# C repeated by DMA instead of TensorE, and a scan that works in place in three PSUM banks

## Chip, cores and metric

The kernel runs on one core of a Trainium2 chip. The metric is the device time of one execution in microseconds. Three runs of the kernel before gave 3733.61, 3746.4 and 3751.59 us; the median is 3746.4.

## What is computed

x is [32, 512, 256] in fp32: 32 sequences of 512 tokens and 256 channels. A macaron block: half a feed-forward, a selective scan, half a feed-forward.

```python
x = x + 0.5 * ffn(layernorm(x), w_gate, w_up, w_down)
x = x + attn(layernorm(x), ...)
x = x + 0.5 * ffn(layernorm(x), w_gate, w_up, w_down)

def ffn(x, w_gate, w_up, w_down):          # 704 hidden; FP4 in blocks of 16, every operand
    return fp4_linear(silu(fp4_linear(x, w_gate)) * fp4_linear(x, w_up), w_down)

def attn(x, W_in, b_in, W_dt1, b_dt1, W_dt2, b_dt2, A, D):     # N = 16 states
    B, C = split(x @ W_in + b_in)
    dt = clip(softplus((x @ W_dt1 + b_dt1) @ W_dt2 + b_dt2), 1e-7, 1e6)
    tmp = A * dt[..., None]
    B_barX = expm1(tmp) / tmp * dt[..., None] * B[:, :, None, :] * x[..., None]
    _, h = associative_scan(combine, (exp(tmp), B_barX), axis=1)   # h = exp(tmp) h_before + B_barX
    return sum(h * C[:, :, None, :], axis=-1) + D * x
```

## The kernel before

Each engine's program is one loop over 34 iterations. Iteration `it` works on several sequences at once: stage A (first feed-forward) and R (norm, projections, dt) for sequence `it`, S (the scan) for `it-1`, C (second feed-forward) for `it-2`, N (norm and quantisation of the next input) for `it+1`. The order in which an engine does the pieces of these stages is a list written out by hand, `ORDER` (lines 27 to 62), with one list for each engine. A word such as `S.w7` is stage, piece and index. Every engine executes its list strictly in order and waits on semaphores in front of each piece, so a piece that waits holds up all that is behind it on its engine. One pass through a list is called a sequence here, and the place where the lists start anew is the seam.

The scan stage works with channels on the 128 partitions, in two groups (G = 2), and tokens along the 512 columns. For each of 16 states n and group gi there is one group m = 2n + gi, 32 in all:

- PE `w` (`differences`, L1303): 12 matmuls of 128x129 write x times the token-to-token differences of B into bank gi of `w_ps`. It waits for the scan that used this bank before.
- ACT `b` (L1103) and POOL `bl` (L495) make the differences of B, ACT `d` (L1115) makes the decay exp(A dt).
- DVE `g` (`state_of`, L787): `tensor_tensor_scan` reads `w_ps` and `decay` and writes `state` in SBUF.
- PE `c` (`repeat_c`, L1313): one matmul of 48x512 repeats row n of C over all 128 partitions into the bank `rep_ps`, from `C_parts`, which holds C as fp16 high part (ACT `ch`, L1067) and low part (DVE `sc`, L760) and is multiplied by a selection matrix `pick_row`.
- DVE `p` (`times_c`, L797): `state` (SBUF) times 1/A times `rep_ps` (PSUM) into `c_state`.
- PE `p` and `e` (`add_y`, L1323): 4 transposing matmuls add `c_state` to `y_ps`.

At the start of a sequence stand k0 and k1, the direct part: PE L1285 writes a product of B, C and D into `w_ps`, DVE L778 multiplies it by x. At the end DVE `y0` (L806) adds `y_ps` to the residual.

Of the feed-forwards these pieces matter: PE `gu` (L1229, 12 matmuls: gate and up), ACT `gu` (L1048, the gate's silu), DVE `hid` (L701, gate times up), DVE `qv` and POOL `qp` (the high and low fp16 parts of the quantised hidden layer), SP `ht` (L416, their transpose by DMA), PE `dn` (L1243, down), DVE `res` (L733, the residual). `N.qy0` and `N.qy1` on DVE (L690) make the next input's fp16 parts, SP `N.tx0` and `N.tx1` (L405) transpose them, and A.gu0 needs them. `R.dt0` (L770, L773) makes dt, `R.xl0` on POOL (L484) the low part of x. `R.cb0` (L752) multiplies B by C from PSUM; `R.rb0` (L1061) takes the projections rows B and C into `rBC`.

PSUM is full: two banks for gate/up, one for the down product, two for `y_ps`, two for `w_ps`, one for `rep_ps`. All DMAs are issued by SP on one queue, in its list's order.

## Time and profile before

| | |
|---|---|
| median of 3 runs | 3746.4 us |
| the profiled execution | 3731.64 us |
| its span, first to last instruction | 3729.6 us |
| mean granted clock of TensorE | 0.966 of full speed |
| busy: PE, DVE, ACT, POOL | 3292.7 (88%), 3399.4 (91%), 2999.9 (80%), 2873.4 us (77%) |
| DMA | 192.07 MB, mean 51 GB/s |

Busy shares are over the whole span. Of its first 200 us a large part goes to the quantisation of the weights and to filling the pipeline, so the work of one sequence is read from a window in the middle. Idle time of an engine in front of a group of instructions is given with what released it; a wait for several semaphores is put down to the one that came last.

### The profile page before, as it was taken

The page shows a single profiled execution, that of the slowest core. Times are in us where ns is not written, and L with a number is a line of the kernel's source. Part 1 is how long each engine was busy: PE and PEld are TensorE (multiplying, and loading weights), DVE is VectorE, ACT ScalarE, POOL GpSimd, SP SyncE. Part 2 cuts the span into 40 slices and gives each one's busy share as a digit, 9 for nine tenths or more (in the row PEclk, how much of TensorE's full clock was granted, in tenths as well). Part 3 has the DMA queues.
Part 4 walks back from the last instruction along what each step waited for, and adds up shares of the span by engine and source line. Part 5 has one row for each costly group of instructions (what it writes and reads, how often), then busy time and mean ns, then how long its engine had stood idle before and what let it go on. Part 6 is the DMA issues. An engine that isn't in the chain of part 4 may idle for free. (4 is left out here: it accounts for less than half of the span.)

```text
span 3729.6 us, 79626 instructions
## 1 busy us (share of the span) xinstructions
PE 3292.7 (88%) x28716; PEld 2351.3 (63%) x28716; DVE 3399.4 (91%) x5419; ACT 2999.9 (80%) x6314; POOL 2873.4 (77%) x2489
## 2 busy tenths in 40 slices
PE   0589999999998999999999999999999999999984
PEld 0256666666666666666666666666666666666663
DVE  5499999999999999999999999999999999999984
ACT  1388888888888888888888888888888888888872
POOL 2458788788877788787878878788888888888854
PEclk9799999999999999999999999999999999999987
DMA  2112222222222222222222222222222222232212
GB/s 37 25 33 49 52 52 54 58 60 46 59 49 51 54 63 47 55 55 49 55 58 61 45 59 49 54 53 60 50 55 60 49 55 54 58 63 43 53 35 43
DMA packets 583023, 192.07 MB, mean 51 GB/s; under 512 B 544039, under 2 KB 578280, under 8 KB 582632
## 3 DMA queue, kind: packets, MB, share of 16 engines
q1 hardware_dynamic: 582632, 186.98, 24.3%
q8 instruction: 230, 3.77, 0.4%
q14 instruction: 161, 1.32, 0.1%
HBM read 19.16 MB, written 16.78 MB: 10 GB/s over the span
## 5 line engine op out<-in xcount | busy, mean ns | idle before, releaser
L787 DVE TENSOR_TENSOR_SCAN state<-w_ps,decay 128x512 f32<-128x512 f32 x1024 | 1210.6, 1208 | 60.3 <-PE w_ps L1303 56.5
L1229 PE MATMUL gu_ps<-wgu,qxT 128*128 128x352 f16 x6144 | 1032.6, 320 | 101.9 <-ACT gate L1048 51.4
L1303 PE MATMUL w_ps<-bdif,x_parts 128*128 128x129 f16 (+1 forms) x12288 | 850.3, 222 | 96.0 <-DVE state L787 88.5
L1303 PEld LDWEIGHTS w_ps<-bdif,x_parts 128*128 128x128 f16 x12288 | 754.0, 98 | 218.4 <-issue 175.3
L1229 PEld LDWEIGHTS gu_ps<-wgu,qxT 128*128 128x128 f16 x6144 | 577.1, 99 | 480.7 <-ACT gate L1048 65.3
L1115 ACT ACTIVATE decay<-dt,A_sb 128x512 f32<-128x512 f32 x1024 | 686.3, 711 | 71.0 <-DVE state L787 43.6
L797 DVE SCALAR_TENSOR_TENSOR c_state<-state,inv_A,rep_ps 128x512 f32<-128x512 f32 x1024 | 723.1, 738 | 7.7 <-issue 3.5
L495 POOL TENSOR_TENSOR bdif<-dif,B_lo 128x516 f16<-128x516 f16 x512 | 535.9, 1060 | 164.7 <-PE w_ps L1303 164.0
L1243 PE MATMUL dn_ps<-wd,qhT 128*128 128x256 f16 (+1 forms) x4608 | 591.6, 279 | 64.0 <-DMA qhT<-qh 62.5
L1323 PE MATMUL y_ps<-ident,c_state 128*128 128x128 f32 x4352 | 621.5, 279 | 22.7 <-DVE c_state L797 22.7
L1103 ACT ACTIVATE bdif<-dif,B_tok 128x129 f16<-128x129 f16 x2048 | 628.9, 393 | 0.0
L1243 PEld LDWEIGHTS dn_ps<-wd,qhT 128*128 128x128 f16 (+1 forms) x4608 | 424.2, 99 | 204.0 <-DMA qhT<-qh 80.3
L1323 PEld LDWEIGHTS y_ps<-ident,c_state 128*128 128x128 f32 x4352 | 470.2, 141 | 121.1 <-issue 81.5
L534 POOL TENSOR_TENSOR val<-val,magic 128x704 f32<-128x704 f32 x256 | 410.5, 1604 | 166.0 <-DVE magic L729 166.0
L1048 ACT ACTIVATE gate<-gu_ps,w_back 128x352 f32<-128x352 f32 x512 | 281.8, 550 | 300.9 <-PE gu_ps L1229 296.6
L542 POOL TENSOR_TENSOR grid<-val,magic 128x704 f16<-128x704 f32 x256 | 444.0, 1735 | 20.1
L526 POOL TENSOR_TENSOR val<-hid,recip 128x704 f32<-128x704 f32 x256 | 378.6, 1494 | 28.3 <-DVE recip L717 27.6
L701 DVE SCALAR_TENSOR_TENSOR hid<-gu_ps,up_back,gate 128x352 f32<-128x352 f32 x512 | 290.2, 567 | 81.2 <-PE gu_ps L1229 65.7
L557 POOL TENSOR_TENSOR qh<-grid,scale_lo 128x704 f16<-128x704 f16 x256 | 354.0, 1388 | 0.4
L1115 ACT ACT_TABLE_LOAD x188 | 241.2, 1283 | 3.3
L724 DVE TENSOR_TENSOR qh<-grid,scale_hi 128x704 f16<-128x704 f16 x256 | 240.7, 940 | 3.2 <-POOL grid L542 3.1
L1039 ACT ACTIVATE magic<-val 128x704 bf16<-128x704 f32 x256 | 197.3, 782 | 39.9 <-POOL val L526 36.0
(160 smaller groups left out, 3803.3 us busy)
## 6 DMA issues: line engine op xcount, KB each, us to landing
x_in<-in_L_attn_x SPq DMA_DIRECT2D x32, 512.0 KB, 3.8
x_s<-x_a SPq DMA_DIRECT2D x32, 512.0 KB, 3.8
out<-x_out SPq DMA_DIRECT2D x32, 512.0 KB, 3.2
qhT<-qh SPq DMA_TRANSPOSE x256, 3.7
qxT<-qx SPq DMA_TRANSPOSE x128, 3.1
hid<-in_L_ffn_w_gate SPq DMA_DIRECT2D x1, 704.0 KB
bdif<-in_L_ffn_w_up SPq DMA_DIRECT2D x1, 704.0 KB
val<-in_L_ffn_w_down SPq DMA_DIRECT2D x1, 704.0 KB, 13.1
```

The lines of the kernel that those rows point to most:

```text
L495: g.tensor_tensor(bdif[:, n % NB, :, 1, 0:P + 1], dif[:, 0:P + 1].unsqueeze(1).broadcast_to([P, T, P + 1]), B_lo[:, seq % 2, :, n:n + 1].b ...
L526: g.tensor_tensor(val[:, t % 2].rearrange("p (b i) -> p b i", i=BLOCK), hid[:, t, :].rearrange("p (b i) -> p b i", i=BLOCK), recip[:, t * ...
L534: g.tensor_tensor(val[:, s], val[:, s], magic[:, s], ALU.add).then_inc(grid_h.sem, 1)
L542: g.tensor_tensor(grid[:, s], val[:, s], magic[:, s], ALU.subtract).then_inc(grid_h.sem, 1)
L787: v.tensor_tensor_scan(state[:, n % 2, gi, :], w_ps[:, gi, :], decay[:, n % 2, gi, :], 0.0, ALU.add, ALU.mult).then_inc(state_ready.sem, 1)
L797: v.scalar_tensor_tensor(c_state[:, n % 2, gi, :], state[:, n % 2, gi, :], inv_A[:, gi, n:n + 1], rep_ps[:], ALU.mult, ALU.mult).then_inc( ...
L1103: last = a.activation(bdif[:, n % NB, t, 0, 0:P + 1], dif[:, 0:P + 1], ACT.Copy, scale=B_tok[:, seq % 2, t, n:n + 1])
L1115: a.activation(decay[:, n % 2, gi, :], dt[:, seq % 2, gi, :], ACT.Exp, scale=A_sb[:, gi, n:n + 1]).then_inc(decay_ready.sem, 1)
L1229: last = te.matmul(gu_ps[:, m, 0:FH], qxT[:, t // 2, 4 * (t % 2) + xp * G + c], wgu[:, c, wp, a:a + FH], start=begin, stop=end)
L1243: last = te.matmul(dn_ps[:], qhT[0:k, t % 2, hp * FC + c, :], wd[0:k, c, wp, :], start=begin, stop=end)
L1303: last = te.matmul(w_ps[:, gi, t * P:t * P + wide], x_parts[:, seq % 2, xp, t, gi * P:(gi + 1) * P], bdif[:, n % NB, t, bp, 0:wide], start ...
L1323: last = te.matmul(y_ps[:, t // 2, col:col + P], c_state[:, n % 2, gi, t * P:(t + 1) * P], ident[:], is_transpose=True, start=(j, t % 2) = ...
```

## The change

C no longer goes through TensorE. Once a sequence SP writes the rows of `rBC` that hold C (16 x 512, fp32) to a scratch in HBM (`C_rows`, two halves in turn), and eight DMAs (`cr0` to `cr7`) read two rows each of it back into all 128 partitions of `C_all` (512 KB each, 4 MB a sequence). `C_parts`, `pick_row`, `is_row`, `rep_ps` and the pieces PE `c`, ACT `ch`, DVE `sc` go. The bank that `rep_ps` held goes to `w_ps`, which has three banks used in turn by the two direct products and the 32 groups (34 uses a sequence). The scan writes its result over its input in the bank, and the product with C reads it from there; `state` goes. A bank is therefore free for PE when the product has been made, not when the scan has. The first product of each pair of states waits for its DMA. All five lists are reordered; of PE's and DVE's the new one is shown whole and of the old one the first and last line; SP's is whole. ScalarE's and GpSimd's are left out of the diff: in them R.xh0 (the fp16 high part of x) moves ahead of R.rb0 and of the softplus, and pieces change places within their stages.

```diff
     "PE": """
-    S.c0 S.k0 S.k1 A.gu0 S.w0 S.w1 S.e0 S.e1 S.w2 A.gu1 A.gu2 S.w3 S.c1 S.p0 S.p1 S.w4 S.w5 A.gu3 S.w6 S.w7 S.p2
...
-    S.w28 S.w29 S.c13 C.dn2 S.w30 S.c14 S.p24 S.p25 S.p26 S.p27 S.w31 S.c15 S.p28 C.dn3 S.p29 S.p30 S.p31
+    S.k0 S.k1 S.w0 S.w1 A.gu0 S.w2 S.w3 S.e0 A.gu1 S.w4 A.gu2 S.e1 S.p0 A.gu3 S.w5 S.w6 S.w7 S.p1 S.p2 S.p3
+    A.gu4 S.p4 S.p5 S.w8 S.w9 S.w10 A.gu5 A.gu6 S.p6 S.p7 A.gu7 C.gu0 S.p8 S.p9 S.w11 S.w12 S.w13 S.p10 C.gu1
+    A.dn0 S.w14 S.w15 S.w16 S.p11 S.p12 A.dn1 C.gu2 S.p13 C.gu3 S.w17 C.gu4 S.p14 S.p15 S.w18 A.dn2 S.w19 S.w20
+    C.gu5 A.dn3 S.w21 C.gu6 S.p16 S.p17 S.p18 C.gu7 S.w22 S.w23 S.p19 S.p20 S.p21 C.dn0 S.w24 S.w25 C.dn1 R.xt0
+    S.w26 S.p22 R.rb0 S.w27 S.w28 R.bt0 S.p23 S.p24 R.z0 C.dn2 S.w29 S.w30 S.w31 S.p25 S.p26 S.p27 S.p28 C.dn3
+    S.p29 S.p30 S.p31
     """,
     "DVE": """
-    S.k0 S.k1 S.g0 S.g1 S.p0 A.hid0 S.p1 C.xa0 C.xa1 A.hid1 C.xs0 A.am0 S.g2 A.hid2 S.g3 S.p2 S.g4 S.p3 C.xm0
...
-    C.res2 S.g29 S.p28 S.p29 S.g30 S.g31 N.qy0 S.p30 S.p31 C.res3 R.dt0 N.qy1 S.y0
+    S.k0 S.k1 S.g0 S.g1 S.p0 S.p1 S.g2 A.hid0 C.xa0 C.xa1 C.xs0 S.g3 A.hid1 C.xm0 A.am0 S.g4 S.p2 A.hid2 S.p3
+    S.p4 C.qy0 A.hid3 C.xm1 A.am1 A.qs0 S.g5 S.g6 S.p5 S.g7 S.p6 S.p7 C.qy1 S.g8 A.hid4 A.qm0 A.qm1 S.g9 A.hid5
+    S.p8 S.p9 S.g10 A.hid6 A.qv0 S.p10 A.hid7 A.am2 A.am3 A.qv1 A.qs1 C.hid0 S.g11 S.g12 S.g13 S.p11 A.qm2 S.p12
+    S.p13 A.qm3 A.res0 S.g14 S.g15 A.qv2 C.hid1 S.p14 S.p15 A.res1 C.hid2 C.am0 S.g16 C.hid3 C.am1 S.g17 C.qs0
+    A.qv3 S.p16 S.p17 C.hid4 C.qm0 A.res2 S.g18 C.qm1 S.p18 S.g19 S.g20 C.hid5 A.res3 S.g21 C.am2 S.p19 S.p20
+    S.p21 C.hid6 C.qv0 C.qv1 C.hid7 C.am3 C.qs1 S.g22 S.g23 S.p22 C.res0 C.qm2 S.g24 S.g25 S.p23 S.p24 C.res1
+    N.xa0 N.xa1 N.xs0 C.qm3 C.qv2 S.p25 S.g26 S.g27 R.tb0 R.cb0 S.g28 S.p26 S.p27 S.p28 C.qv3 N.xm0 N.xm1 S.g29
+    C.res2 S.g30 S.g31 S.p29 S.p30 S.p31 C.res3 R.dt0 N.qy0 N.qy1 S.y0
     """,
...
     "SP": """
-    S.keep0 C.tx0 C.tx1 A.ht0 A.ht1 A.ht2 A.ht3 N.load0 C.ht0 C.ht1 C.ht2 C.ht3 N.tx0 N.tx1 C.store0
+    S.keep0 C.tx0 C.tx1 S.cr5 S.cr6 A.ht0 A.ht1 A.ht2 A.ht3 N.load0 C.ht0 C.ht1 S.cr7 C.ht2 C.ht3 R.cw0 C.store0
+    N.tx0 N.tx1 R.cr0 R.cr1 R.cr2 R.cr3 R.cr4
     """,
...
     PR = ROW_C + N
-    KC = 3 * N
     NB = 4
+    BANKS = 3
...
         y_ps = psum("y_ps", [P, G, L])
-        w_ps = psum("w_ps", [P, 2, L])
-        rep_ps = psum("rep_ps", [P, L])
+        w_ps = psum("w_ps", [P, BANKS, L])
...
         B_lo = sb("B_lo", [P, 2, T, N], F16)
-        C_parts = sb("C_parts", [P, 2, L], F16)
+        C_all = sb("C_all", [P, N, L])
+        C_rows = nc.dram_tensor("C_rows", [2, N, L], F32, kind="Internal").ap()
         CB = sb("CB", [ROW_B + N + 1, L])
         rBC = sb("rBC", [PR, L])
         soft = sb("soft", [P, G, L])
         dt = sb("dt", [P, 2, G, L])
         bdif = sb("bdif", [P, NB, T, 2, WIDE], F16)
         decay = sb("decay", [P, 2, G, L])
-        state = sb("state", [P, 2, G, L])
         c_state = sb("c_state", [P, 2, G, L])
         consts_in = count("consts_in")
...
         dt_ready = count("dt_ready", G + 1)
-        rep_full = count("rep_full", N)
+        C_out = count("C_out", 16)
+        C_in = [count("C_in_%d" % k, 16) for k in range(N // 2)]
...
+        def w_bank(seq, u):
+
+            return w_ps[:, (seq * (G + G * N) + u) % BANKS, :]
+
         gu_flat = gu_ps[:].rearrange("p a b -> p (a b)")
         block = ctx.enter_context(nc.Block())
...
+            def keep_C(seq):
+
+                sp.wait_ge(r_ready.sem, r_ready.at(seq, 1))
+                if before(seq, 2):
+                    for k in range(N // 2):
+                        sp.wait_ge(C_in[k].sem, C_in[k].at(seq - 2, 16))
+                sp.dma_start(C_rows[seq % 2], rBC[ROW_C:PR, :]).then_inc(C_out.sem, 16)
+
+            def repeat_C(seq, k):
+
+                sp.wait_ge(C_out.sem, C_out.at(seq, 16))
+                if not first(seq):
+                    sp.wait_ge(c_state_ready.sem, c_state_ready.at(seq - 1, G + 2 * G * k + 2 * G))
+                sp.dma_start(C_all[:, 2 * k:2 * k + 2, :],
+                             C_rows[seq % 2, 2 * k:2 * k + 2, :].unsqueeze(0).broadcast_to([P, 2, L])
+                             ).then_inc(C_in[k].sem, 16)
+
             def body(it, pieces, pass_a, pass_c, pass_n):
                 q = {"A": pass_a, "C": pass_c, "N": pass_n}
                 for stage, step, k in pieces:
-                    if step == "tx":
+                    if step == "cw":
+                        keep_C(it)
+                    elif step == "cr" and stage == "R":
+                        repeat_C(it, k)
+                    elif step == "cr":
+                        repeat_C(it - 1, k)
+                    elif step == "tx":
                         turn_x(q[stage], k)
                     elif step == "ht":
                         turn_h(q[stage], k)
...
                 dve.wait_ge(w_ready.sem, w_ready.at(seq, gi + 1))
-                v.tensor_tensor(c_state[:, 1, gi, :], xT[:, gi, :], w_ps[:, gi, :], ALU.mult).then_inc(c_state_ready.sem, 1)
+                v.tensor_tensor(c_state[:, 1, gi, :], xT[:, gi, :], w_bank(seq, gi), ALU.mult).then_inc(c_state_ready.sem, 1)
             def state_of(seq, m):
                 n, gi = m // G, m % G
                 dve.wait_ge(decay_ready.sem, decay_ready.at(seq, m + 1))
-                if n >= 2:
-                    dve.wait_ge(c_state_ready.sem, c_state_ready.at(seq, m - G + 1))
                 dve.wait_ge(w_ready.sem, w_ready.at(seq, G + m + 1))
-                v.tensor_tensor_scan(state[:, n % 2, gi, :], w_ps[:, gi, :], decay[:, n % 2, gi, :], 0.0,
+                v.tensor_tensor_scan(w_bank(seq, G + m), w_bank(seq, G + m), decay[:, n % 2, gi, :], 0.0,
                                      ALU.add, ALU.mult).then_inc(state_ready.sem, 1)
             def times_c(seq, m):
...
                 if gi == 0:
-                    dve.wait_ge(rep_full.sem, rep_full.at(seq, n + 1))
+                    dve.wait_ge(C_in[n // 2].sem, C_in[n // 2].at(seq, 16))
                 dve.wait_ge(state_ready.sem, state_ready.at(seq, m + 1))
-                v.scalar_tensor_tensor(c_state[:, n % 2, gi, :], state[:, n % 2, gi, :], inv_A[:, gi, n:n + 1], rep_ps[:],
+                v.scalar_tensor_tensor(c_state[:, n % 2, gi, :], w_bank(seq, G + m), inv_A[:, gi, n:n + 1], C_all[:, n, :],
                                        ALU.mult, ALU.mult).then_inc(c_state_ready.sem, 1)
             def take_y(seq, pass_c):
...
                 act.wait_ge(rB_ps.sem, rB_ps.at(seq, 1))
+                if not first(seq):
+                    act.wait_ge(C_out.sem, C_out.at(seq - 1, 16))
                 a.activation(rBC[:], gu_ps[0:PR, 0, :], ACT.Identity, bias=b_rBC[0:PR, :]).then_inc(r_ready.sem, 1)
-
-            def high_C(seq):
-                act.wait_ge(rB_ps.sem, rB_ps.at(seq, 1))
-                if before(seq, 2):
-                    act.wait_ge(rep_full.sem, rep_full.at(seq - 2, N))
-                a.activation(C_parts[0:N, seq % 2, :], gu_ps[ROW_C:PR, 0, :], ACT.Identity,
-                             bias=b_C[0:N, :]).then_inc(C_hi.sem, 1)
             def softplus(seq):
...
                         pe.wait_ge(CB_ready.sem, CB_ready.at(seq, 1))
-                        pe.wait_ge(C_lo.sem, C_lo.at(seq, 1))
                     te.matmul(gu_ps[:, gi, :], W_dt2_sb[:, gi * P:(gi + 1) * P], rBC[0:R, :], start=True,
                               stop=True).then_inc(z_ps.sem, 1)
+            def bank_free(seq, u):
+
+                uses = seq * (G + G * N) + u - BANKS
+                if uses >= 0:
+                    pe.wait_ge(c_state_ready.sem, uses + 1)
+
             def direct(seq, gi):
                 if gi == 0:
                     pe.wait_ge(CB_ready.sem, CB_ready.at(seq, 1))
-                    if not first(seq):
-                        pe.wait_ge(state_ready.sem, state_ready.at(seq - 1, G * N))
-                te.matmul(w_ps[:, gi, :], AD[ROW_B:ROW_B + N + 1, gi * P:(gi + 1) * P], CB[ROW_B:ROW_B + N + 1, :], start=True,
+                bank_free(seq, gi)
+                te.matmul(w_bank(seq, gi), AD[ROW_B:ROW_B + N + 1, gi * P:(gi + 1) * P], CB[ROW_B:ROW_B + N + 1, :], start=True,
                           stop=True).then_inc(w_ready.sem, 1)
...
                     pe.wait_ge(x_lo.sem, x_lo.at(seq, 1))
                 pe.wait_ge(b_hi_ready.sem, b_hi_ready.at(seq, n + 1))
                 pe.wait_ge(b_lo_ready.sem, b_lo_ready.at(seq, n + 1))
-                if n:
-                    pe.wait_ge(state_ready.sem, state_ready.at(seq, m - G + 1))
-                else:
-                    pe.wait_ge(c_state_ready.sem, c_state_ready.at(seq, gi + 1))
+                bank_free(seq, G + m)
+                bank = w_bank(seq, G + m)
                 for t in range(T):
                     wide = P + (t < T - 1)
                     for xp, bp in PARTS:
-                        last = te.matmul(w_ps[:, gi, t * P:t * P + wide], x_parts[:, seq % 2, xp, t, gi * P:(gi + 1) * P],
+                        last = te.matmul(bank[:, t * P:t * P + wide], x_parts[:, seq % 2, xp, t, gi * P:(gi + 1) * P],
                                          bdif[:, n % NB, t, bp, 0:wide], start=(t, xp, bp) == (0, 0, 0),
                                          stop=(t, xp) == (T - 1, 1), skip_group_check=True)
                 last.then_inc(w_ready.sem, 1)
-
-            def repeat_c(seq, n):
-                if n:
-                    pe.wait_ge(c_state_ready.sem, c_state_ready.at(seq, G + G * n))
-                else:
-                    pe.wait_ge(C_lo.sem, C_lo.at(seq, 1))
-                te.matmul(rep_ps[:], pick_row[:, n, :], C_parts[0:KC, seq % 2, :], start=True, stop=True).then_inc(rep_full.sem, 1)
             def add_y(seq, j):
```

The prologue loses the making of `is_row` and `pick_row` (DVE), the clearing of `C_parts` (POOL) and two small loads; `w_val`, a buffer of the weights' quantisation, moves from `state` to `C_all`.

## Rows read from the trace of the kernel before

**Rows 1.** Busy time by engine, 400 to 3500 us: us (instructions), granted clock, DMA
```profile
core 0: us, PE busy (x) PEld busy (x) DVE busy (x) ACT busy (x) POOL busy (x), PEclk, DMA share, GB/s
400.00:3500.00 3100.00, 2878.18 (x25413) 2063.79 (x25412) 2934.53 (x4706) 2656.30 (x5584) 2530.89 (x2184) 0.98 0.26 54
```

**Rows 2.** Groups of instructions, 400 to 3500 us: busy, mean ns, idle before, releasers
```profile
L787 DVE TENSOR_TENSOR_SCAN state<-w_ps,decay 128x512 f32<-128x512 f32 x908 | 1073.4, 1208 | 50.5 <-PE w_ps L1303 48.4 <-ACT decay L1115 2.1
...
L1303 PE MATMUL w_ps<-bdif,x_parts 128*128 128x129 f16 (+1 forms) x10908 | 751.7, 222 | 79.3 <-DVE state L787 75.4 <-DVE c_state L778 3.8
...
L797 DVE SCALAR_TENSOR_TENSOR c_state<-state,inv_A,rep_ps 128x512 f32<-128x512 f32 x908 | 641.3, 738 | 5.7 <-issue 2.7 <-PE rep_ps L1313 1.7
...
L701 DVE SCALAR_TENSOR_TENSOR hid<-gu_ps,up_back,gate 128x352 f32<-128x352 f32 x457 | 258.9, 567 | 55.6 <-PE gu_ps L1229 40.5 <-ACT gate L1048 13.4 <-issue 0.2
...
L1313 PE MATMUL rep_ps<-C_parts,pick_row 48*128 48x512 f16 x453 | 177.0, 391 | 7.1 <-DVE c_state L797 7.1
...
L733 DVE SCALAR_TENSOR_TENSOR x_out<-dn_ps,down_back,x_c 128x256 f32<-128x256 f32 x112 | 53.3, 476 | 28.7 <-PE dn_ps L1243 28.5
...
L760 DVE SCALAR_TENSOR_TENSOR C_parts<-gu_ps,b_C,C_parts 16x512 f16<-16x512 f32 x28 | 21.1, 753 | 0.9
...
L773 DVE TENSOR_SCALAR dt<-dt 128x1024 f32<-128x1024 f32 x28 | 19.4, 694 | 1.0
```

**Rows 3.** Timeline of DVE around four seams: start, us, instruction, idle before
```profile
837.77 2.34 DVE L787 TENSOR_TENSOR_SCAN state<-w_ps,decay 128x512 f32<-128x512 f32 x2 [0.50 <-PE w_ps L1303]
...
945.40 2.34 DVE L787 TENSOR_TENSOR_SCAN state<-w_ps,decay 128x512 f32<-128x512 f32 x2 [0.50 <-PE w_ps L1303]
...
1045.85 2.07 DVE L690 TENSOR_TENSOR qx<-x_grid,x_scale_hi 128x512 f16<-128x512 f16 x1
...
1059.19 2.34 DVE L787 TENSOR_TENSOR_SCAN state<-w_ps,decay 128x512 f32<-128x512 f32 x2 [3.21 <-PE w_ps L1303]
...
1606.06 0.40 DVE L690 TENSOR_TENSOR qx<-x_grid,x_scale_hi 128x512 f16<-128x512 f16 x1
...
1611.02 0.42 DVE L806 SCALAR_TENSOR_TENSOR x_c<-y_ps,x_s 128x256 f32<-128x256 f32 x1
...
1614.17 2.34 DVE L787 TENSOR_TENSOR_SCAN state<-w_ps,decay 128x512 f32<-128x512 f32 x2 [0.50 <-PE w_ps L1303]
```

**Rows 4.** Timeline of PE around two seams, columns as in rows 3
```profile
1049.82 1.31 PE L1323 MATMUL y_ps<-ident,c_state 128*128 128x128 f32 x8 [2.03 <-DVE c_state L797]
...
1054.09 3.70 PE L1229 MATMUL gu_ps<-wgu,qxT 128*128 128x352 f16 x12
...
1610.99 1.96 PE L1229 MATMUL gu_ps<-wgu,qxT 128*128 128x352 f16 x12
```

**Rows 5.** Busy time by engine in a stretch at a slow seam, columns as in rows 1
```profile
1055.00:1060.00 5.00, 5.00 (x37) 3.72 (x36) 1.79 (x3) 4.81 (x12) 4.51 (x8) 0.57 0.77 247
```

**Rows 6.** Groups of instructions, whole span, columns as in rows 2
```profile
L778 DVE TENSOR_TENSOR c_state<-xT,w_ps 128x512 f32<-128x512 f32 x64 | 41.0, 680 | 0.7 <-PE w_ps L1285 0.7
...
L1076 ACT ACTIVATE soft<-gu_ps,b_dt_sb 128x512 f32<-128x512 f32 x64 | 40.5, 684 | 0.8
...
L1080 ACT ACTIVATE gu_ps<-gu_ps,b_dt_sb 128x512 f32<-128x512 f32 x64 | 39.7, 658 | 1.0
...
L910 DVE TENSOR_TENSOR state<-hid,recip 88x1024 f32<-88x1024 f32 x2 | 2.4, 1218 | 0.0
...
L910 DVE TENSOR_TENSOR state<-val,recip 128x704 f32<-128x704 f32 x2 | 1.7, 890 | 0.0
```

**Rows 7.** Timeline of SP's DMA issues at the seam, columns as in rows 3
```profile
1611.13 1.23 SPq L405 DMA_TRANSPOSE qxT<-qx  x1
```

**Rows 8.** DMA issues of the whole span: count, KB each, median us to landing
```profile
x_in<-in_L_attn_x SPq DMA_DIRECT2D x32, 512.0 KB, 3.8
...
b_C<-in_L_attn_b_in SPq DMA_DIRECT2D x3, 0.1 KB, 1.6
W_rBC<-in_L_attn_W_in SPq DMA_DIRECT2D x2, 16.0 KB, 2.1
...
b_in_all<-in_L_attn_b_in SPq DMA_DIRECT2D x1, 16.0 KB, 3.5
```

More of the change, by code:

```diff
@@ L28 @@
     "PE": """
-    S.c0 S.k0 S.k1 A.gu0 S.w0 S.w1 S.e0 S.e1 S.w2 A.gu1 A.gu2 S.w3 S.c1 S.p0 S.p1 S.w4 S.w5 A.gu3 S.w6 S.w7 S.p2
-    S.c2 A.gu4 A.gu5 S.c3 S.w8 S.p3 S.p4 S.w9 A.gu6 S.p5 S.c4 S.p6 A.gu7 C.gu0 S.w10 S.w11 S.p7 S.c5 S.p8 S.p9
-    S.w12 C.gu1 A.dn0 S.w13 C.gu2 S.c6 S.w14 S.w15 C.gu3 S.p10 A.dn1 C.gu4 S.w16 S.w17 S.p11 A.dn2 S.p12 C.gu5
-    S.c7 A.dn3 S.c8 S.p13 C.gu6 S.w18 C.gu7 S.c9 S.p14 S.w19 S.w20 S.p15 S.p16 S.p17 C.dn0 S.w21 S.w22 C.dn1
-    S.w23 S.c10 R.xt0 S.w24 S.w25 R.rb0 S.c11 S.p18 S.p19 R.bt0 S.p20 S.w26 S.c12 S.p21 S.w27 S.p22 S.p23 R.z0
@@ L35 @@
+    S.w26 S.p22 R.rb0 S.w27 S.w28 R.bt0 S.p23 S.p24 R.z0 C.dn2 S.w29 S.w30 S.w31 S.p25 S.p26 S.p27 S.p28 C.dn3
+    S.p29 S.p30 S.p31
     """,
     "DVE": """
-    S.k0 S.k1 S.g0 S.g1 S.p0 A.hid0 S.p1 C.xa0 C.xa1 A.hid1 C.xs0 A.am0 S.g2 A.hid2 S.g3 S.p2 S.g4 S.p3 C.xm0
-    S.g5 C.xm1 S.g6 A.hid3 A.am1 A.qs0 A.hid4 S.p4 S.p5 S.g7 A.hid5 C.qy0 C.qy1 A.qm0 A.qm1 S.p6 S.p7 S.g8 S.g9
-    A.hid6 S.p8 S.p9 A.hid7 A.am2 A.am3 A.qs1 A.qv0 S.g10 S.g11 C.hid0 S.p10 S.p11 A.qm2 A.qm3 S.g12 A.qv1
-    C.hid1 S.g13 C.am0 A.res0 A.qv2 C.hid2 S.p12 S.g14 S.g15 C.hid3 C.am1 A.res1 S.p13 C.qs0 A.qv3 S.g16 S.g17
@@ L41 @@
-    C.qm0 C.hid4 A.res2 C.qm1 C.hid5 S.p14 S.p15 C.am2 C.qv0 A.res3 C.hid6 S.p16 S.p17 S.g18 C.hid7 C.qv1 C.am3
-    C.qs1 S.g19 S.g20 C.res0 S.p18 S.p19 C.qm2 S.g21 S.g22 C.res1 S.g23 S.p20 S.p21 S.g24 S.g25 N.xa0 N.xa1
-    S.p22 S.p23 R.tb0 N.xs0 C.qm3 C.qv2 R.sc0 R.cb0 S.p24 S.g26 S.g27 S.p25 S.g28 S.p26 S.p27 C.qv3 N.xm0 N.xm1
-    C.res2 S.g29 S.p28 S.p29 S.g30 S.g31 N.qy0 S.p30 S.p31 C.res3 R.dt0 N.qy1 S.y0
+    S.k0 S.k1 S.g0 S.g1 S.p0 S.p1 S.g2 A.hid0 C.xa0 C.xa1 C.xs0 S.g3 A.hid1 C.xm0 A.am0 S.g4 S.p2 A.hid2 S.p3
@@ L298, in macaron_program @@
         r_ready = count("r_ready", 1)
-        C_hi = count("C_hi", 1)
-        C_lo = count("C_lo", 1)
         B_ps = count("B_ps", 1)
@@ L372, in _ @@
             sp.dma_start(b_rBC[ROW_C:PR, :], column(b_in[N:2 * N])).then_inc(bc_in.sem, 16)
-            for k in (0, 2 * N, ROW_B):
-                sp.dma_start(b_C[k:k + N, :], column(b_in[N:2 * N])).then_inc(bc_in.sem, 16)
+            sp.dma_start(b_C[ROW_B:ROW_B + N, :], column(b_in[N:2 * N])).then_inc(bc_in.sem, 16)
             sp.dma_start(W_dt2_sb[:], W_dt2).then_inc(consts_in.sem, 16)
@@ L820, in body @@
                         times_B(it)
-                    elif step == "sc":
-                        low_C(it)
                     elif step == "k":
@@ L882, in _ @@
             body(-1, order("DVE", "N"), None, None, 0)
-            w_val = state[:].rearrange("p a g l -> p (a g l)")
+            w_val = C_all[:, 0:2 * G, :].rearrange("p n l -> p (n l)")
             w_magic = decay[:].rearrange("p a g l -> p (a g l)").bitcast(BF16)
@@ L1143, in body @@
                         take_rBC(it)
-                    elif step == "ch":
-                        high_C(it)
                     elif step == "xh":
@@ L1343, in body @@
                         differences(seq, k)
-                    elif step == "c":
-                        repeat_c(seq, k)
                     elif step == "e":
```

49 lines of the change are left out of this document (18 added, 31 removed).

## The prediction

> **What bounds the kernel now.** I read first what each engine does between 400 and 3500 us, where the pipeline is full: VectorE (DVE) is busy 2934.5 of 3100 us (94.7%), TensorE (PE) 2878.2 (92.8%), ScalarE 86%, GpSimd 82% [rows 1]. Next the groups of instructions in that window. The `dt` clamp (L773) runs once a sequence and 28 times there, so a sequence takes 110.7 us: 104.8 of DVE work and 5.9 of DVE idle time, against 102.8 of PE work. DVE sets the pace, PE is close behind. A microsecond taken from DVE's work or idle time counts; one taken from PE counts only where DVE waits for PE.
>
> The last part of each line says what DVE waited for: 48.4 us for the differences in `w_ps`, 40.5 and 13.4 for the gate/up matmuls and the gate, 28.5 for the down matmuls, only 1.7 for the repeated C. PE in turn waits 75.4 us for scans to free a bank [rows 2].
>
> The 48.4 us lie at the seam between two sequences, and seams come in two kinds [rows 3]. At 1614.17 the first scan waited 0.50 us, at 1059.19 it waited 3.21. Of the 28 seams 9 wait 3.2 us or more, 5 wait 1.7 to 2.1, the rest 0.5 or less. A slow one begins on DVE: the N.qy0 instruction at 1045.85 takes 2.07 us where the one at 1606.06 takes 0.40. The products behind it are late and PE sits idle 2.03 us for them. Then 12 gate/up matmuls take 3.70 us, where 12 take 1.96 at the other seam [rows 4], and the granted clock of that stretch is 0.57, most of it at 1.2 instead of 2.4 GHz [rows 5]. The old list puts these 12 (A.gu0) ahead of w0 and w1.
>
> **The change, part by part, per sequence.**
>
> *C no longer by TensorE.* The `repeat_c` matmuls hold PE for 177.0 us [rows 2], 6.3 a sequence; they overlap with their neighbours a little, so I count 5. C's high half on ScalarE goes, where there is idle time: nothing. On DVE the low half goes, 21.1 us busy in 28 sequences. **-0.8 us.**
>
> *Scan in place, product from PSUM.* Each scan now writes PSUM. Each product reads PSUM as its first tensor and SBUF as its second, where it was the other way round, so it still has one tensor from each. No row shows DVE writing a result to PSUM. The nearest [rows 6]: ScalarE's Relu in place in PSUM takes 658 ns, its Abs from PSUM to SBUF 684, so PSUM as target is 26 ns cheaper there. On DVE, products wholly in SBUF take 890 ns for 704 and 1218 for 1024 elements, 1.025 each plus 168, hence 693 for 512; the product with a PSUM operand takes 680, so a PSUM read costs nothing. That one and the product with C (738, [rows 2]) differ by 58 ns at one size, my upper bound; -26 is the lower. I take 0, nearest to the in-place row. Over 1024 scans the bounds are -27 and +59 us.
>
> The Trainium skill (VectorE: DVE Perf Modes, section on the TRN2 errata) gives a PSUM source 62 cycles more fixed cost than an SBUF source. The 680 against 693 ns of this trace shows none of it for a read; for a write no run here shows it. Charged to every scan it would be, as an estimate, 65 ns x 1024 = 66 us.
>
> *Three banks instead of two, held until the product.* PE may write group m+3 once product m is done, where it could write m+2 once scan m was. A round is the 12 matmuls (751.7 us for 909 groups, 0.83), the scan (1.18), the product (0.71) and, as my estimate, two handovers of 0.2: 3.1 us, or 1.0 a group with three banks. DVE has 110.7/32 = 3.5 us a group. So banks bind only in bursts. I walked the new lists: w3 waits for p0, w17 for p14, w28 for p25, and each time DVE has over 2 us of other work before the scan that needs it. Cost 0 on DVE; if that cover is gone, it is rival (d).
>
> *The seam.* New PE order: k0, k1, w0 (its bank is free since p31), w1, A.gu0, w2, w3. w0 is there before DVE comes. w1 waits for the first direct product and is done 1.0 us after it; DVE wants it 1.8 us after (one more direct product, one scan). g2 wants w2 4.2 us after the first direct product; it is there after 0.2 + 0.83 + 1.96 + 0.83 = 3.8 at full clock, and with these matmuls at half clock 2.5 us late. From a mean of 1.7 us now (48.4/28) I keep 0.6. **-1.1 us.**
>
> *Gate/up waits.* 53.9 us in the window, 1.9 a sequence, where PE is late in its list. PE has 5 us less to do; I take off half. **-0.9 us.** The wait for the down matmuls (1.0) hangs on a transpose's landing and stays.
>
> *C's way through the scratch.* The 32 KB write is issued after C.ht3, a dozen DVE instructions before the repeats. Then come eight transfers of 512 KB. By the lists cr5 to cr7 are issued well ahead of their products. cr0 is not: it stands behind N.tx1 on SP's queue. That issue starts when N.qy1 is done, at 1611.13, and takes 1.23 us [rows 7], so cr0 is issued 1.3 to 1.4 us after N.qy1's end. It lands 3.8 us later, as the 512 KB of `x_in` from HBM do [rows 8]: 5.2 us after N.qy1. DVE is at p0 after y0, k0, k1 and two scans, from 1611.02 to 1614.17 + 2.34, less 0.50 of waiting: 5.0 us [rows 3]. **+0.2 us.** cr1 to cr4 follow at once and are wanted some 10 us of DVE work apart. C.store0, now ahead of N.tx0, waits for C.res3, 3 us earlier in DVE's list than N.qy1. C.tx0 comes some 16 us into the next sequence behind 2.6 MB; at the 247 GB/s of [rows 5] (DMA share 0.77, so not full) they are gone after 11. Bounds: nothing (C there in time), and rival (a).
>
> *Sum.* -0.8 - 1.1 - 0.9 + 0.2 = -2.6 us a sequence, times 31 that have a seam before or after them = -81. The few constants dropped ahead of the loop I count at nothing, since the weights' chain covers them. **-81 us.** The profiled execution took 3731.6 us (span 3729.6 and 2.0 around it): 3651. The median of the three runs is 3746.4, 15 us above it; on that footing **3665 us**.
>
> **Rivals.** *(a) The broadcast lands late (slower).* All 128 rows of a repeat read the same 4 KB of HBM. With a landing of L us the first product waits L + 1.4 - 5.0, and at L = 6.4 it has eaten the gain. The one broadcast shown, b_in to 128 partitions, 16 KB, landed in 3.5 us where W_in's 16 KB took 2.1; 0.1 KB takes 1.6 [rows 8]. So `x_in`'s 3.8 is 1.6 fixed and 2.2 for the data. If the data part is three times as long, L = 8.2, the wait 4.6 instead of 0.2, +136 us: 3801. Against it: b_in was issued behind other loads. Later repeats would still be in time.
>
> The Trainium skill (DMA: Bandwidth & Descriptors, section Latency and other measured facts) tells of copies whose streams step together onto the same HBM channels and fall to half their rate. No run here shows it. With the data part doubled L = 6.0 and the wait is 2.4, and by that rule the time would be 3733.
>
> *(b) Every seam goes cold (no change).* PE has 5 us more idle time a sequence. At the seam I count, from the lists, 1.5 us before C.dn3 (its transpose lands late) and 1.8 before w1, near the 2.03 after which the clock fell. A sequence without a cold seam takes 107.6 us (837.77 to 945.40), the next one 113.8 (945.40 to 1059.19) [rows 3]. If all go cold the mean rises from 110.7 by 2 to 3 us, times 31 = 62 to 93: 3727 to 3758.
>
> *(c) The scan pays for PSUM.* +59 us: 3724, about no change. *(d) Bank waits spread (slower).* PE stops in its list for a product that DVE does late, with the gate/up matmuls behind it. It decides from 0.08 us a group; at 0.12 it is 32 x 31 x 0.12 = +119: 3784. *(e) More of the idle time goes*: 3.0 of the 5.9 us, and the 0.8: 3746 - 118 = 3628.
>
> **How the numbers follow.** No change means within 0.5%, 3728 to 3765, about what a measurement of this kernel can tell. Forecast 0.45 and (e) 0.12: faster. (b) 0.16 and (c) 0.07: no change, but for 0.05 of them just beyond on the fast side. (a) 0.13 and (d) 0.07: slower, but for 0.02 where the landing is a little late. Faster 0.62, same 0.20, slower 0.18. The forecast's own range is 3638 to 3705 (-27 for the write; the gate's waits kept whole, +28, and 0.4 us more at the seam, +12). The range for all goes from a little under (e), 3615, to 3785, which leaves out the worse half of (a).
>
> **What would show it.** No DVE instruction for C's low half, none of PE on `rep_ps`; the scan's mean within 20 ns of 1208; the first scan's wait at the seam 0.5 us or less; the first product waiting 0.2 us for `C_all`'s DMA (2 or more is rival a) and its landing 3 to 4 us; PE busy near 90% of a full stretch, with more waits for `c_state`; a period of 108.1 us. I am wrong if the clock in full stretches is granted below 0.95 (b), if the scan takes 1240 ns or more (c), or if the gate's waits grow (d).

## The result, and the profile after

The changed kernel takes **3850.9 us** (median, 3846.7 to 3866.3); before, in the same comparison, 3740.0. The comparison gives a ratio of 1.034 (95% interval 1.029 to 1.039); the quotient of the two medians alone is 1.030. The forecast was 3665, its range 3615 to 3785: wrong in sign and out of range. The profiled execution has a span of 3849.9 us against 3729.6, and a mean granted clock of 0.946 against 0.966.

The page's row of busy times, over the whole span:

```profile
PE 3155.9 (82%) x28204; PEld 2355.3 (61%) x28204; DVE 3402.8 (88%) x5385; ACT 2977.3 (77%) x6282; POOL 2840.4 (74%) x2488
```

DVE works as long as before (3402.8 against 3399.4 us). PE works 137 us less. All of the loss is idle time on DVE: the shares below add up to it. The groups of DVE from 400 to 3500 us (columns as in [rows 2]):

```profile
L796 DVE TENSOR_TENSOR_SCAN w_ps<-w_ps,decay 128x512 f32<-128x512 f32 x874 | 1037.9, 1213 | 54.4 <-ACT decay L1117 27.1 <-PE w_ps L1305 25.9 <-issue 0.2
L806 DVE SCALAR_TENSOR_TENSOR c_state<-w_ps,inv_A,C_all 128x512 f32<-128x512 f32 x873 | 612.1, 736 | 46.2 <-DMA C_all<-C_rows 45.3
L721 DVE SCALAR_TENSOR_TENSOR hid<-gu_ps,up_back,gate 128x352 f32<-128x352 f32 x438 | 245.7, 561 | 23.5 <-PE gu_ps L1229 16.2 <-ACT gate L1055 0.5 <-issue 0.2
...
L682 DVE TENSOR_REDUCE x_amax<-f_xh 128x32 f32<-128x512 f32 x110 | 72.4, 680 | 7.6 <-ACT f_xh L1028 7.6
L753 DVE SCALAR_TENSOR_TENSOR x_a<-dn_ps,down_back,x_in 128x256 f32<-128x256 f32 x108 | 51.2, 474 | 89.5 <-PE dn_ps L1243 89.5
L753 DVE SCALAR_TENSOR_TENSOR x_out<-dn_ps,down_back,x_c 128x256 f32<-128x256 f32 x108 | 50.7, 469 | 5.7 <-PE dn_ps L1243 5.4
...
L700 DVE TENSOR_SCALAR x_magic<-x_magic 128x512 bf16<-128x512 bf16 x110 | 29.3, 286 | 11.9 <-ACT x_magic L1042 11.7
```

The window holds 874 scans, 27.3 sequences, where it held 908 before, 28.4. Divided by these, DVE's idle time per sequence went from 5.8 to 9.7 us. Where the 3.9 come from, idle time after less idle time before in us a sequence, against [rows 2] and, for what those don't list (x_a, x_magic and x_amax were under 0.1, decay 0.1), the same view of before:

| DVE waits for | change |
|---|---|
| the down matmuls, at x_a | +3.3 |
| C's transfer, at the product | +1.7 |
| ScalarE's decay, at the scan | +0.9 |
| ScalarE's x_magic and f_xh | +0.7 |
| the gate/up matmuls and the gate, at hid | -1.1 |
| the down matmuls, at x_out | -0.8 |
| `w_ps`, at the scan | -0.8 |

3.9 x 31 sequences are 121 us; the span grew by 120.3. The scan takes 1213 ns (1208 in [rows 2]), the product 736 (738).

PE's groups of the same window say what x_a's matmuls wait for:

```profile
L1305 PE MATMUL w_ps<-bdif,x_parts 128*128 128x129 f16 x10488 | 711.6, 224 | 86.1 <-DVE c_state L789 63.4 <-DVE c_state L806 21.8 <-POOL bdif L517 0.5
L1243 PE MATMUL dn_ps<-wd,qhT 128*128 128x256 f16 (+1 forms) x3888 | 517.7, 285 | 116.9 <-DMA qhT<-qh 114.4
```

The down matmuls wait 114.4 us for the transposes of the hidden layer. The timeline of SP's queue over one seam and the middle of the next sequence shows why:

```profile
1541.64 2.59 SPq L405 DMA_TRANSPOSE qxT<-qx  x2
1544.33 2.70 SPq L432 DMA_DIRECT2D C_all<-C_rows  x5
...
1562.38 17.88 SPq L405 DMA_TRANSPOSE qxT<-qx  x2
1580.35 1.01 SPq L432 DMA_DIRECT2D C_all<-C_rows  x2
1581.46 27.13 SPq L416 DMA_TRANSPOSE qhT<-qh  x4
```

C.tx0 is issued at 1562.38, C.tx1 only at 1579.03, when the gate/up matmuls have freed its buffer (the row shows the two as one, 17.88 us to the end of the second). cr5 and cr6 stand behind it, so these 1 MB go out at 1580.35, and the first transpose of the hidden layer is issued 1.1 us after them, at 1581.46. On PE and DVE, in the same stretch:

```profile
1584.10 1.95 PE L1229 MATMUL gu_ps<-wgu,qxT 128*128 128x352 f16 x12
1589.59 3.81 PE L1243 MATMUL dn_ps<-wd,qhT 128*128 128x256 f16 x18 [3.54 <-DMA qhT<-qh]
...
1596.28 2.23 PE L1243 MATMUL dn_ps<-wd,qhT 128*128 128x256 f16 x18
```

```profile
1541.87 0.41 DVE L710 TENSOR_TENSOR qx<-x_grid,x_scale_lo 128x512 f16<-128x512 f16 x1
...
1548.42 1.41 DVE L806 SCALAR_TENSOR_TENSOR c_state<-w_ps,inv_A,C_all 128x512 f32<-128x512 f32 x2 [1.31 <-DMA C_all<-C_rows]
...
1593.54 0.48 DVE L753 SCALAR_TENSOR_TENSOR x_a<-dn_ps,down_back,x_in 128x256 f32<-128x256 f32 x1 [4.01 <-PE dn_ps L1243]
```

The landing of `qhT` (the time from issue until the data are there), 3.2 us in the median of all, reaches 8.7; this one takes 8.1. PE idles 3.54 us, 18 down matmuls then take 3.81 us (the next 18 shown take 2.23; the granted clock from 1590 to 1595 is 0.71), and x_a waits 4.01. At the seam the first product waits 1.31 us for C.

### The profile page after: what moved, and what is told of

It reads as the page before. It is cut to its first block and busy times, and to the rows that moved or that the text cites. A ratio compares the mean times of both kernels' runs of the same rounds, so it can differ in the third digit from the quotient of the medians.

```text
span 3849.9 us, 79124 instructions
## 1 busy us (share of the span) xinstructions
PE 3155.9 (82%) x28204; PEld 2355.3 (61%) x28204; DVE 3402.8 (88%) x5385; ACT 2977.3 (77%) x6282; POOL 2840.4 (74%) x2488
## 5 line engine op out<-in xcount | busy, mean ns | idle before, releaser
L796 DVE TENSOR_TENSOR_SCAN w_ps<-w_ps,decay 128x512 f32<-128x512 f32 x1024 | 1215.7, 1213 | 65.3 <-ACT decay L1117 32.9
L1229 PE MATMUL gu_ps<-wgu,qxT 128*128 128x352 f16 x6144 | 1082.8, 325 | 194.5 <-DVE hid L721 89.4
L1305 PE MATMUL w_ps<-bdif,x_parts 128*128 128x129 f16 (+1 forms) x12288 | 838.5, 225 | 126.2 <-DVE c_state L789 71.1
L806 DVE SCALAR_TENSOR_TENSOR c_state<-w_ps,inv_A,C_all 128x512 f32<-128x512 f32 x1024 | 717.6, 736 | 53.6 <-DMA C_all<-C_rows 52.4
L1243 PE MATMUL dn_ps<-wd,qhT 128*128 128x256 f16 (+1 forms) x4608 | 626.1, 289 | 160.5 <-DMA qhT<-qh 155.5
L517 POOL TENSOR_TENSOR bdif<-dif,B_lo 128x516 f16<-128x516 f16 x512 | 555.3, 1099 | 135.8 <-PE w_ps L1305 135.8
L1318 PE MATMUL y_ps<-ident,c_state 128*128 128x128 f32 x4352 | 571.0, 274 | 17.3 <-DVE c_state L806 17.3
L564 POOL TENSOR_TENSOR grid<-val,magic 128x704 f16<-128x704 f32 x256 | 412.1, 1610 | 20.1
L548 POOL TENSOR_TENSOR val<-hid,recip 128x704 f32<-128x704 f32 x256 | 363.1, 1440 | 5.8 <-DVE recip L737 5.7
L535 POOL TENSOR_TENSOR x_val<-x_val,x_magic 128x512 f32<-128x512 f32 x128 | 148.5, 1160 | 204.1 <-DVE x_magic L700 204.1
L527 POOL TENSOR_TENSOR x_val<-f_xh,x_recip 128x512 f32<-128x512 f32 x128 | 194.0, 1526 | 81.2 <-DVE x_scale_hi L692 81.2
```

The costliest lines, as they stand in the source:

```text
L517: g.tensor_tensor(bdif[:, n % NB, :, 1, 0:P + 1], dif[:, 0:P + 1].unsqueeze(1).broadcast_to([P, T, P + 1]), B_lo[:, seq % 2, :, n:n + 1].b ...
L548: g.tensor_tensor(val[:, t % 2].rearrange("p (b i) -> p b i", i=BLOCK), hid[:, t, :].rearrange("p (b i) -> p b i", i=BLOCK), recip[:, t * ...
L564: g.tensor_tensor(grid[:, s], val[:, s], magic[:, s], ALU.subtract).then_inc(grid_h.sem, 1)
L796: v.tensor_tensor_scan(w_bank(seq, G + m), w_bank(seq, G + m), decay[:, n % 2, gi, :], 0.0, ALU.add, ALU.mult).then_inc(state_ready.sem, 1)
L806: v.scalar_tensor_tensor(c_state[:, n % 2, gi, :], w_bank(seq, G + m), inv_A[:, gi, n:n + 1], C_all[:, n, :], ALU.mult, ALU.mult).then_inc ...
L1229: last = te.matmul(gu_ps[:, m, 0:FH], qxT[:, t // 2, 4 * (t % 2) + xp * G + c], wgu[:, c, wp, a:a + FH], start=begin, stop=end)
```

## Experiments

Each is compared with the kernel before in runs of the same chip; its medians there were 3733.2 (e1 to e4), 3732.5 (e5 to e8), 3729.5 (e9 to e11) and 3729.1 us (e12). Waits are those of 400 to 3500 us.

**Where the repeats stand in SP's list: e1 to e3.**

```diff
 e1:
-    S.keep0 C.tx0 C.tx1 S.cr5 S.cr6 A.ht0
+    S.keep0 S.cr5 S.cr6 C.tx0 C.tx1 A.ht0
 e2:
-    N.tx0 N.tx1 R.cr0 R.cr1
+    R.cr0 N.tx0 N.tx1 R.cr1
 e3: both
```

> Theory: in the changed kernel cr5 and cr6 are issued in SP's list between C.tx1 and A.ht0; C.tx1 waits until the previous pass has left its buffer, so these 1 MB go out just ahead of A.ht0, its transpose lands late, PE stops at A.dn0 and DVE at A.res0 (91.3 us of waiting in the window, 3.3 a sequence). Here cr5 and cr6 stand right behind S.keep0. Expected: that wait falls to 0.5 us a sequence or less, time 3850 - 31 x 3 = about 3757 (3740 to 3775), the wait for C_all stays near 1.7 us a sequence. Rival (the order of DVE and PE around A.dn0 is itself too tight, whatever the DMA): the wait stays above 2 us a sequence and the time within 20 us of 3850. Second rival (the queue is overfull at the seam): the wait moves to C_all, by as much.

Measured: 3733.1 us, ratio 0.9996 (0.9976 to 1.0016). x_a's wait is gone (89.5 to 0.0), C's wait at the seam stays (45.2). **Two words in a list are the whole loss, 118 us**, more than was expected: x_a's wait is 102 of it (3.3 a sequence, 31 times), and with it the waits for `w_ps` (25.9 to 13.1) and in front of hid (23.5 to 13.0) get shorter.

> Only cr0 is moved, from behind N.tx1 to ahead of N.tx0 on SP's queue. Theory: the first product waits for C_all only because cr0 is issued behind N.tx1 (1.6 us a sequence); the wait goes, DVE's wait at A.res0 stays at 3.3 us: 3850 - 50 = about 3800. Rival: DVE has to wait elsewhere for the same time (w0 to w2 late, gate/up waits at the seam because N.tx0 lands later): above 3835.

Measured: 3829.8 us, 1.0272 (1.0242 to 1.0302), between the 3800 expected and the rival's 3835: only 21 us better than after. Its groups:

```profile
L796 DVE TENSOR_TENSOR_SCAN w_ps<-w_ps,decay 128x512 f32<-128x512 f32 x874 | 1038.5, 1214 | 92.0 <-PE w_ps L1305 63.7 <-ACT decay L1117 27.0 <-issue 0.2
L806 DVE SCALAR_TENSOR_TENSOR c_state<-w_ps,inv_A,C_all 128x512 f32<-128x512 f32 x875 | 613.4, 736 | 0.9
```

C's wait is gone, but the scan's wait for `w_ps`, 25.9 in after, is 63.7. The wait for C had covered PE's lateness.

> Both moves. Theory: the two waits are separate and add up: 3850 - 93 - 50 = about 3707, that is 0.99 of the kernel before. If they overlap or their time goes to the next wait (decay, w_ps), 3740 to 3760, no faster than before.

Measured: 3723.5 us, 0.9983 (0.9961 to 1.0006), between the two times given. With both transfers in their places the change is worth 0.2%, which can't be told from nothing, and not the 2.2% forecast. So the rest of the forecast was wrong too.

**No repeats after the first sequence: e4.** The kernel leaves them out, and the products don't wait for them.

```diff
             def repeat_C(seq, k):
...
+                if not first(seq):
+                    return
...
-                if gi == 0:
+                if gi == 0 and first(seq):
```

> This kernel leaves out the eight repeats of C for all sequences but the first, so every sequence uses the first one's C; all else, the lists and the writes to the scratch too, is as in the changed kernel. It takes all of the repeats' traffic and waits away. Theory (traffic and its place in the queue are the whole loss): both waits go, the time is at or below that of the run with both moves, 3690 to 3710. Rival (the lists and the three banks lose by themselves): it stays above 3760 though no repeat is in flight.

Measured: 3717.2 us, 0.9958 (0.9934 to 0.9981), a little less good than expected. Some 6 us of e3's time are the repeats' own. In e3 the transfers no longer hold the change back; what does is in the engines: their lists, or the third bank.

**What the seam costs.** PE over the seam in e3_both, and the same stretch by windows (columns: us, busy time of PE, PEld, DVE, ACT, POOL with their instructions, granted clock, DMA share, GB/s):

```profile
1592.08 0.86 PE L1305 MATMUL w_ps<-bdif,x_parts 128*128 128x129 f16 x12
1595.44 1.45 PE L1305 MATMUL w_ps<-bdif,x_parts 128*128 128x129 f16 x12 [2.51 <-DVE c_state L789]
1596.69 3.73 PE L1229 MATMUL gu_ps<-wgu,qxT 128*128 128x352 f16 x12
1600.21 1.93 PE L1305 MATMUL w_ps<-bdif,x_parts 128*128 128x129 f16 x24
```

```profile
1590.00:1595.00 5.00, 2.93 (x19) 1.35 (x16) 4.96 (x16) 4.61 (x9) 1.66 (x4) 0.92 0.85 232
1595.00:1600.00 5.00, 4.55 (x24) 3.03 (x25) 4.53 (x6) 4.89 (x12) 4.60 (x7) 0.50 1.10 272
```

w0 is made early, as forecast, but w1 needs the bank of the first direct product, and PE idles 2.51 us for it. Then A.gu0 runs at a granted clock of 0.50 (1.2 GHz): 12 matmuls in 3.73 us against 1.96, and w2, behind it, comes 2.03 us too late. In the timeline of PE from 400 to 3500 us this is at each of the 28 seams: idle 1.7 to 2.5 us, then 2.8 to 3.7 for A.gu0. Before, it was at some [rows 3, 4]. DVE's groups of e3:

```profile
L796 DVE TENSOR_TENSOR_SCAN w_ps<-w_ps,decay 128x512 f32<-128x512 f32 x906 | 1076.8, 1214 | 84.0 <-PE w_ps L1305 55.1 <-ACT decay L1117 27.7 <-issue 0.2
...
L734 DVE TENSOR_SCALAR scale<-amax,h_min 128x88 f32<-128x88 f32 x114 | 56.3, 494 | 2.0
...
L692 DVE TENSOR_SCALAR x_scale_hi<-x_scale 128x64 bf16<-128x64 f32 x57 | 26.5, 466 | 0.0
L784 DVE TENSOR_SCALAR dt<-dt 128x1024 f32<-128x1024 f32 x28 | 24.6, 880 | 1.0
```

Per sequence the scan waits 1.9 us for `w_ps`, a little more than before (1.7), and 1.0 for decay d4, which ScalarE makes behind x_magic and its wait for GpSimd.

**Moving pieces of the lists, on e3: e6 to e9.**

```diff
 e6, ACT and DVE:
-    S.b3 A.gu1 C.ax0 S.d4 A.gu2        S.g3 A.hid1 C.xm0 A.am0 S.g4 S.p2 A.hid2
+    S.b3 A.gu1 S.d4 A.gu2 C.ax0        S.g3 A.hid1 A.am0 S.g4 S.p2 A.hid2 C.xm0
 e7, PE and DVE:
-    S.w1 A.gu0 S.w2 S.w3               S.g2 A.hid0 C.xa0 C.xa1 C.xs0 S.g3
+    S.w1 S.w2 A.gu0 S.w3               S.g2 C.xa0 C.xa1 C.xs0 A.hid0 S.g3
 e8: e6 and e7
 e9: e7, and ACT:
-    S.d3 A.gu0 C.ln0 S.b2 S.b3 A.gu1 C.ax0 S.d4 A.gu2
+    S.d3 S.d4 C.ln0 A.gu0 S.b2 S.b3 A.gu1 C.ax0 A.gu2
```

> On e3_both: ScalarE makes decay d4 ahead of x_magic (C.ax0), which comes behind the third gate; VectorE's C.xm0 moves behind A.hid2. Theory S (e3's idle time is the new lists' doing: ScalarE holds d4's table load and the gate behind x_magic, which waits 2.6 us for GpSimd, so the scan waits 0.94 for decay, x_magic 0.4, and 12 gate/up matmuls run at half clock in 3.5 us after TensorE waited 2.4 for the gate): the scan's waits for decay fall from 28 to under 5 us in 400 to 3500, hid's do not grow, 2.0 us a sequence, 3665 (3650 to 3690). Rival T (the idle time only moves to the next wait, since another engine is late by as much): over 3705.

Measured: 3727.5 us, 0.999 (0.9968 to 1.0012): a miss, rival T.

```profile
L796 DVE TENSOR_TENSOR_SCAN w_ps<-w_ps,decay 128x512 f32<-128x512 f32 x906 | 1074.3, 1212 | 44.3 <-PE w_ps L1305 42.2 <-ACT decay L1117 0.6 <-issue 0.2
...
L710 DVE TENSOR_TENSOR qx<-x_grid,x_scale_hi 128x512 f16<-128x512 f16 x114 | 85.7, 752 | 37.7 <-POOL x_grid L539 37.7
```

The wait for decay is gone. But C.xm0, moved back, makes GpSimd's x_grid late: C.qy0 waits 37.7 us for it and takes 752 ns instead of 452: in the timeline it falls on GpSimd's next instruction (1.62 us at 1617.63, beside one that runs from 1617.46 to 1618.97).

> On e3_both: TensorE's A.gu0 stands behind w2 instead of ahead of it, and VectorE's A.hid0 behind C.xs0. Theory S (with three banks w1 waits for the first direct product, TensorE is idle 2.5 us at every seam, and A.gu0 then runs at half clock, 3.7 us, ahead of w2): the scan g2 no longer waits (w_ps waits from 55 to under 25 us in 400 to 3500), the price moves to A.hid0 only in part, since the x_amax reduces stand ahead of it: 1.0 to 1.8 us a sequence, 3670 to 3695. Rival T (A.hid0 and what follows wait by as much): 3715 to 3735.

Measured: 3689.4 us, 0.9876 (0.9846 to 0.9906): theory S. The scan's wait for `w_ps` falls from 55.1 to 14.6; the waiting for f_xh at x_amax grows from 7.7 to 31.4.

> The list changes of e6 and e7 together on e3_both. Theory S: they add up, 3 to 3.8 us a sequence: 3610 to 3640, faster than before by 2.5 to 3 per cent; the granted clock from 400 to 3500 over 0.97. Rival T: over 3690.

Measured: 3731.0 us, 0.9993 (0.9975 to 1.0011): a miss, by e6's step (x_grid 37.8 again).

> On e7_gu0_late: ScalarE makes d4 right behind d3 and C.ln0 ahead of the first gate. Theory S (what is left of the new lists' idle time is ScalarE's order at the seam): the scan's waits for decay (22 us in 400 to 3500) and those of x_amax for f_xh (31) fall to under 10 together, and two table loads a sequence go; hid may wait up to 1 us more a sequence. 0.7 to 1.5 us a sequence: 3643 to 3668. Rival T (as in e8_both_lists, the order moves the wait onto GpSimd's x_grid or to the gates): 3680 or more.

Measured: **3651.7 us, 0.9775 (0.9731 to 0.9819)**, faster than both kernels and inside the range given. ScalarE's table loads fall as forecast, by two a sequence (172 and 144 in e7 to 145 and 115). DVE's groups, and PE at a seam:

```profile
L796 DVE TENSOR_TENSOR_SCAN w_ps<-w_ps,decay 128x512 f32<-128x512 f32 x928 | 1101.1, 1213 | 10.8 <-PE w_ps L1305 9.1 <-issue 0.3
...
L721 DVE SCALAR_TENSOR_TENSOR hid<-gu_ps,up_back,gate 128x352 f32<-128x352 f32 x464 | 261.4, 563 | 25.3 <-ACT gate L1055 18.7 <-PE gu_ps L1229 2.3 <-issue 0.4
...
L682 DVE TENSOR_REDUCE x_amax<-f_xh 128x32 f32<-128x512 f32 x113 | 73.7, 675 | 6.6 <-ACT f_xh L1028 6.5
```

```profile
1572.70 1.99 PE L1305 MATMUL w_ps<-bdif,x_parts 128*128 128x129 f16 x24 [2.42 <-DVE c_state L789]
1574.49 3.19 PE L1229 MATMUL gu_ps<-wgu,qxT 128*128 128x352 f16 x12
```

PE still idles 2.42 us and A.gu0 still runs cold here (3.19 us; 1.95 to 3.65 over the seams), but w1 and w2 are ahead of it, and DVE has x_amax to do meanwhile.

**The queue or the bytes: e10, e11, on the kernel after.**

```diff
 e10:
-    C.tx1 S.cr5 S.cr6 A.ht0
+    C.tx1 S.cr5 S.cr6 S.cr7 A.ht0
 e11: SP, and ACT:
-    C.tx1 S.cr5 S.cr6 A.ht0            A.gu7 C.gu0
+    C.tx1 A.ht0                        A.gu7 S.cr5 S.cr6 C.gu0
```

> The kernel after, with cr7 also ahead of A.ht0: 1.5 MB instead of 1 MB on SP's queue between C.tx1 and the hidden layer's transposes. Theory F (the transposes wait for the bytes ahead of them): each further 512 KB holds A.ht0 back by what one costs now, half of the 3.3 us that x_a waits a sequence, but no less than 1.3 us (512 KB at 400 GB/s): x_a's wait for dn_ps from 89.5 to 125 to 160 us in 400 to 3500, the time 3890 to 3925. Rival G (the cost is the change of kind on the queue, from copies to transposes, whatever the bytes): as after, 3840 to 3860.

In this kernel cr7 no longer stands behind C.ht1. Measured: 3908.2 us, 1.0462 (1.0418 to 1.0506), theory F:

```profile
L753 DVE SCALAR_TENSOR_TENSOR x_a<-dn_ps,down_back,x_in 128x256 f32<-128x256 f32 x108 | 51.2, 474 | 139.0 <-PE dn_ps L1243 139.0
```

5.2 us a sequence (858 scans, 26.8 sequences) against 3.3: 1.9 us for a further 512 KB, and 57 us in all. A.ht0 lands 8.2 us after its issue in the median of the seams, against 7.5 in after and 3.2 in e1.

> The kernel after, with cr5 and cr6 issued by ScalarE's queue behind its seventh gate, about when SP issues them now; SP's list has A.ht0 right behind C.tx1. The same bytes at about the same time. Theory F (first in, first out on SP's queue is what costs): A.ht0 goes ahead at once and shares the DMA engines; x_a's wait from 89.5 to under 35 us in 400 to 3500, the wait at the seam for C_all stays: 3735 to 3780. Rival B (it is the bytes, on whatever queue): x_a's wait stays over 60, 3815 or more. Two DMA issues on ScalarE cost it some 0.1 us and a wait at most.

Measured: 3753.4 us, 1.0053 (1.0025 to 1.0081), inside theory F's range.

```profile
L753 DVE SCALAR_TENSOR_TENSOR x_a<-dn_ps,down_back,x_in 128x256 f32<-128x256 f32 x112 | 53.0, 473 | 16.3 <-PE dn_ps L1254 16.3
```

But the trace doesn't bear theory F out. The issues at a seam, and how many us each took to land:

```profile
1538.50 0.81 ACTq L1071 DMA_DIRECT2D C_all<-C_rows  x2
...
1539.63 1.23 SPq L405 DMA_TRANSPOSE qxT<-qx  x1
1542.00 2.76 SPq L416 DMA_TRANSPOSE qhT<-qh  x1
```

```profile
C_all<-C_rows ACTq DMA_DIRECT2D x2, 512.0 KB, 5.1
qxT<-qx SPq DMA_TRANSPOSE x1, 7.2
qhT<-qh SPq DMA_TRANSPOSE x1, 6.2
```

The copies don't go out at the same time: they are issued 3.5 us ahead of A.ht0, where SP issued them 1.1 us ahead. And the transposes don't pass them on their own queue. C.tx1, issued 1.1 us after the copies, lands after 7.2 us where it took 2.7 in after, ahead of them; A.ht0 takes 6.2, against 8.1 in after and 3.2 in e1 (medians of the seams: C.tx1 6.2 against 2.7; A.ht0 6.1, 7.5 and 3.2). Between 1539.5 and 1542.5 the trace has packets of ScalarE's queue alone. So what e11 gains goes with the head start of 2.4 us, and with the clock: here PE waits 1.56 us for the transpose instead of 3.54, and the 18 down matmuls behind it take 2.24 us instead of 3.81. That another queue helps by itself isn't shown. The Trainium skill (DMA: Bandwidth & Descriptors, section Queues, rings and completion order) says that each DMA engine works down a ring in order and takes turns between rings, a whole packet of descriptors at a time; e1 and e10 agree with the order, a turn for SP's ring doesn't show in e11 until the copies are nearly through.

**C by DMA alone: e5.** The kernel before with its own lists, two banks and `state` in SBUF; only the repeats are by DMA.

```diff
-                v.scalar_tensor_tensor(c_state[...], state[...], inv_A[...], rep_ps[:],
+                v.scalar_tensor_tensor(c_state[...], state[...], inv_A[...], C_all[:, n, :],
```

> C through the scratch alone: the kernel before with its own lists, two banks and the scan writing SBUF, only repeat_c and C's high and low half taken out and the transfers put in (cr5, cr6 ahead of C.tx0, cr0 ahead of N.tx0). Theory P (DVE and GpSimd disturb each other when a DVE product has all its operands in SBUF, and that is why the scan had to move to PSUM): the product, 738 ns with rep_ps, takes over 800 ns or its GpSimd neighbours grow; 1024 products, so 3780 or more. Theory Q (no such contention, C by DMA pays by itself what was forecast for it: 0.8 for the low half and part of 0.9 for the gate/up waits, nothing at the seam, 31 times): product within 20 ns of 738, 3680 to 3705. Theory R (what TensorE gives up is of no use to VectorE, and the cold seams become more): 3715 to 3745.

Measured: 4247.7 us, 1.1369 (1.1335 to 1.1403), theory P, and far beyond 3780.

```profile
L809 DVE SCALAR_TENSOR_TENSOR c_state<-state,inv_A,C_all 128x512 f32<-128x512 f32 x786 | 1001.8, 1303 | 0.8
L799 DVE TENSOR_TENSOR_SCAN state<-w_ps,decay 128x512 f32<-128x512 f32 x786 | 926.6, 1203 | 84.7 <-PE w_ps L1312 83.9
```

The product takes 1303 ns instead of 738; 1024 times 0.565 us are 579, more than the 515 that the kernel loses. Two pairs of products and what GpSimd did meanwhile:

```profile
1507.83 3.19 DVE L809 SCALAR_TENSOR_TENSOR c_state<-state,inv_A,C_all 128x512 f32<-128x512 f32 x2
...
1524.02 1.38 DVE L809 SCALAR_TENSOR_TENSOR c_state<-state,inv_A,C_all 128x512 f32<-128x512 f32 x2
```

```profile
1507.64 1.05 POOL L518 TENSOR_TENSOR bdif<-dif,B_lo 128x516 f16<-128x516 f16 x1
1508.65 3.60 POOL L580 TENSOR_TENSOR qh<-grid,scale_lo 128x704 f16<-128x704 f16 x2
...
1523.91 1.02 POOL L501 TENSOR_TENSOR f_rstd<-f_var,minus_half 128x4 f32<-128x4 f32 x1
```

Beside GpSimd's large instructions two products take 3.19 us, beside its 4-element one 1.38. GpSimd suffers as well: its `qh` takes 1707 ns where it took 1381. The Trainium skill (SBUF — State Buffer, section Who interferes with whom) says that a DVE instruction with two inputs in SBUF and a GpSimd instruction that reads SBUF shut each other out; the trace agrees. So the scan in place in PSUM isn't an extra: with it the product has one input in PSUM and takes 736 ns, and C in SBUF is bearable.

**The same care for the kernel before: e12.**

```diff
-    S.k1 A.gu0 S.w0 S.w1 S.e0          S.p0 A.hid0 S.p1 C.xa0 C.xa1 A.hid1 C.xs0
+    S.k1 S.w0 S.w1 A.gu0 S.e0          S.p0 S.p1 C.xa0 C.xa1 C.xs0 A.hid0 A.hid1
-    S.d2 A.gu0 C.ln0 A.gu1
+    S.d2 C.ln0 A.gu0 A.gu1
```

> A control: the kernel before, C still by TensorE, with the same care in its lists as e9 gives the changed kernel: A.gu0 behind w0 and w1 instead of ahead of them, x_amax (C.xa0, C.xa1, C.xs0) ahead of A.hid0, ScalarE's C.ln0 ahead of the first gate. Theory U (e9's gain is in large part what any careful seam would give): the scan's w_ps waits from 48 to about 14 us in 400 to 3500 (0.5 at every seam), the hid waits no longer than now: 3690 to 3715. Theory V (the gain needs the change: here TensorE has nothing to do between k1 and the first direct product, 2 us, then w0, w1 and A.gu0 run at half clock, and with two banks and the repeats in its list it doesn't catch up): the hid or x_amax waits grow by as much as the scan's fall: 3725 to 3770.

Measured: 3783.2 us, 1.0166 (1.011 to 1.0222), theory V and worse than its range.

```profile
L787 DVE TENSOR_TENSOR_SCAN state<-w_ps,decay 128x512 f32<-128x512 f32 x896 | 1061.5, 1208 | 43.4 <-PE w_ps L1303 30.1 <-ACT decay L1115 11.4
...
L701 DVE SCALAR_TENSOR_TENSOR hid<-gu_ps,up_back,gate 128x352 f32<-128x352 f32 x448 | 253.9, 567 | 87.2 <-PE gu_ps L1229 71.1 <-ACT gate L1048 15.6
```

The scan's wait falls from 48.4 to 30.1, hid's rises from 40.5 and 13.4 [rows 2] to 71.1 and 15.6. An order like the one that pays in the changed kernel costs here (with two banks w2 would have to wait for the first scan, so A.gu0 still stands ahead of it, and d4 was not moved). Other orders of the old lists weren't tried, so it isn't shown that e9's time is out of the old kernel's reach.

## Why the prediction was wrong, step by step

**C's way through the scratch: the step that failed, 118 us.** "By the lists cr5 to cr7 are issued well ahead of their products" is true, and asks the wrong question. The sum had +0.2 us a sequence for the whole of C's way, all of it at the first product, and nothing for anyone else on the queue. I looked at who waits for the transfer, and at C.tx0, but not at who stands behind it on the queue: A.ht0 to A.ht3. Nor did I see that cr5 and cr6, behind C.tx1, can't leave before the gate/up matmuls let that go, just when the transposes are due. "The wait for the down matmuls (1.0) hangs on a transpose's landing and stays" fails with it: in front of x_a it went from 0.0 to 3.3. e1 gives the price, e10 its growth with the bytes; e11 shows that transposes issued shortly after these copies land late from another queue too.

**C's wait at the first product: +0.2 forecast, 1.7 measured.** Both of its terms were too small. N.tx0 and N.tx1 stand back to back and take 2.59 us together, where I took one of 1.23: cr0 leaves 2.1 us after N.qy1's end at 1542.3, not 1.3 to 1.4. And it lands 4.1 us after its issue at this seam, 4.0 to 5.5 over all (median 4.3), not 3.8. Rival (a) is refuted: the 128-fold read is hardly slower than `x_in` (3.9 in this trace), neither two nor three times. Most of the 1.7 was also cover for PE's lateness (e2, e3).

**The seam: -1.1 forecast.** Without the cover it is +0.2 (e3). Rival (b)'s mechanism came true: I had w2 2.5 us late with PE at half clock, 6.7 us after the first direct product; in e3 that product ends at about 1595.2 (two end at 1595.9) and the scan starts at 1601.56, 6.4 us after it, having waited 2.03. I had seen 1.8 us of idle time before w1, and still took the full clock as likelier. Its price of 62 to 93 us did not come: from -1.1 to +0.2 are 1.3 us a sequence, 40 us in all. It stood on a period of 110.7 us, counted by 28 `dt` clamps; 908 scans make it 109.2.

**Gate/up waits, -0.9:** right in size (-1.1; -1.5 in e3). That it is PE's spare time, and not the new order, no run separates. **The wait for the down matmuls at x_out:** it fell by 0.8.

**C's low half, -0.8 x 31 = -25:** gone, but DVE's busy time didn't fall, 3399.4 to 3402.8. In the new order small instructions on SBUF fall beside GpSimd's: x_scale_hi takes 466 ns in e3 and took 131, the `dt` clamp 880 (694), `scale` 494 (317, and still 311 in after). One x_scale_hi of e3 takes 0.84 us from 1572.79, and GpSimd's `qh`, running since 1572.21, ends at 1573.58; its fastest takes 0.13. I costed pieces that are moved at nothing.

**ScalarE's list: nothing forecast, +1.6** for decay, x_magic and f_xh. Its list was reordered too, and my sum had no term for it.

**Scan in place, 0:** right. 1213 ns against 1208, 5 us in all; with the result in SBUF it takes 1203 in e5. Rival (c) is refuted, and of the 66 us worked out beside the Trainium skill (VectorE: DVE Perf Modes, section on the TRN2 errata) no more than these 5 show. **Three banks, 0:** right but for w1 at the seam.

The terms side by side, in us a sequence from 400 to 3500 (e3 has 28.3 sequences there):

| | forecast | e3 less before |
|---|---|---|
| DVE's busy time | -0.8 | +0.8 |
| `w_ps` at the scan | -1.1 | +0.2 |
| in front of hid | -0.9 | -1.5 |
| the down matmuls, at x_out | 0 | -0.7 |
| C at the product | +0.2 | -0.2 |
| ScalarE's decay, x_magic, f_xh | 0 | +1.6 |
| sum | -2.6 | +0.2 |

So of the -81 forecast e3 shows -10 in its median, within what can't be told from nothing, and 118 of the loss is one step. Even those 10 us don't lie in the full stretch.

## What to carry to other kernels

A transfer put into a queue is costed by what stands behind it there, and by what stands ahead of it and holds it until then, not only by its consumer. Issue it well before the transfers that others wait for (e1: 34 us before, no wait); another queue alone was not shown to help (e11). When a wait is taken away, ask whose lateness it covered. Two inputs in SBUF on DVE beside a busy GpSimd can cost more than the engine time that a move to SBUF saves: keep one of them in PSUM.

## What the runs showed that was not expected

- The lockout between DVE and GpSimd: 738 to 1303 ns for the product (717 to 2011 in single ones), in a kernel that takes 14% longer (e5).
- Down matmuls behind a wait of 3.54 us take 3.81 us for 18, and 2.23 a little later: a late transfer is paid a second time in the clock.
- A transpose issued on SP's queue 1.1 us after 1 MB of copies on ScalarE's took 7.2 us to land, where it takes 2.7 with no copy ahead (e11, after).
- A broadcast of 512 KB from HBM to 128 partitions lands in 4.1 us when it is alone (cr7 at 1626.2), a plain load of that size in 3.9. All repeats of a full stretch take 5.6 in the median; five of a sequence's eight are issued one behind the other.
